# A routed block of convolution, attention and experts: b1 in a constant channel, GELU in two halves, both 16-bit casts on ScalarE

## The reference

```python
x = x + conv_block(group_norm(x))         # 3x3 depthwise, BN, ReLU, prune; 1x1, BN, ReLU, prune
t = tokens(x)                             # 12544 tokens of 128 channels
t = t + spike_attention(layer_norm(t))    # causal, within an image of 784 tokens
flat = layer_norm(t)
logits = flat @ Wr                        # 8 experts, the best two of each token
for e in range(8):
    hdn = gelu(flat @ W1[e] + b1[e])      # 128 -> 512, exact GELU
    y = hdn @ W2[e] + b2[e]               # 512 -> 128
    out += gates[:, e:e+1] * y
```

## Time and profile before

| | us |
|---|---|
| median of 3 runs | 878.62 |
| the three runs | 872.77, 878.62, 881.32 |
| the profiled execution, its own time | 872.08 |
| its span, first to last instruction | 870.4 |
| TensorE busy in it | 714.3 (82%) |
| VectorE busy | 658.5 (76%) |
| GpSimd busy | 512.9 (59%) |
| ScalarE busy | 413.2 (47%) |
| mean granted TensorE clock | 0.926 of full |

### The profile page before, as it was taken

The page is one execution under the profiler, slowest core; times in us unless marked ns, Lnnn a source line. Parts: engine busy times, 40 slices in busy tenths (PEclk is TensorE's granted clock), DMA queues, the critical chain, the costliest instruction groups (busy, mean ns, idle before and its releaser), DMA issues. The chain is left out here.

```text
span 870.4 us, 21192 instructions
## 1 busy us (share of the span) xinstructions
PE 714.3 (82%) x6445; PEld 554.3 (64%) x6445; DVE 658.5 (76%) x1980; ACT 413.2 (47%) x922; POOL 512.9 (59%) x500
## 2 busy tenths in 40 slices
PE   1579999999999999798488977669999999995433
PEld 0245666666566666566377866658899999994322
DVE  2647888888888887877759867747888888885666
ACT  0245465566665666455456544335555555552000
POOL 4100057777767776676556677777677777776000
PEclk9989999999999999999679998889999999998555
DMA  7201213232323232122163333325854454441997
GB/s 161 61 19 61 63 59 97 90 113 90 112 88 117 93 117 70 31 73 70 51 108 79 74 76 70 79 72 126 106 95 93 95 95 88 89 84 48 292 306 260
DMA packets 123065, 86.44 MB, mean 99 GB/s; under 512 B 96492, under 2 KB 105232, under 8 KB 122979
## 3 DMA queue, kind: packets, MB, share of 16 engines
q1 hardware_dynamic: 106066, 52.86, 26.2%
q0 software_dynamic: 13888, 26.03, 10.5%
q10 hardware_dynamic: 3024, 6.43, 2.0%
HBM read 30.50 MB, written 35.48 MB: 76 GB/s over the span
## 5 line engine op out<-in xcount | busy, mean ns | idle before, releaser
L477 POOL DMA_INDIRECT expert_rows<-xb_x,dest x210 | 230.5, 1098 | 83.6 <-issue 53.1
L466 POOL DMA_INDIRECT dispatched_rows<-rows,pos x224 | 216.9, 968 | 95.9 <-issue 66.0
L720 PE MATMUL pair_d<-w,xb_x 128*128 x2520 | 177.4, 222 | 0.1
L521 PE MATMUL pair_a<-padx,tap_diag 128*128 128x392 f16 x864 | 164.7, 338 | 0.9 <-ACT h L802 0.9
L720 PEld LDWEIGHTS pair_d<-w,xb_x 128*128 128x128 f16 x2520 | 157.9, 99 | 5.7 <-issue 0.2
L1305 DVE TENSOR_TENSOR xb_x<-seen_g,xb_x 128x512 f16<-128x512 f32 x210 | 137.3, 693 | 0.0
L521 PEld LDWEIGHTS pair_a<-padx,tap_diag 128*128 128x128 f16 x864 | 83.6, 100 | 58.0 <-issue 3.9
L884 ACT ACTIVATE seen_g<-pair_b,b 128x256 f32<-128x256 f32 x212 | 83.4, 477 | 63.7 <-PE pair_b L704 50.0
L884 ACT ACTIVATE seen_g<-pair_c,b 128x256 f32<-128x256 f32 x208 | 82.0, 477 | 34.9 <-PE pair_c L704 33.8
L1302 DVE CAST xb_x<-seen_g 128x512 f16<-128x512 f32 x210 | 84.6, 444 | 0.4 <-ACT seen_g L884 0.3
L704 PE MATMUL pair_b<-xrt,w 128*128 128x256 f16 x636 | 80.6, 278 | 3.4 <-DMA xrt<-dispatched_rows 3.4
(11 more groups left out here) (208 smaller groups left out, 1127.0 us busy)
## 6 DMA issues: line engine op xcount, KB each, us to landing
xb_x<-in_x SPq DMA_DIRECT2D x32, 392.0 KB, 4.2
w<-expert_rows SPq DMA_DIRECT2D x16, 784.0 KB, 6.5
t_all<-t SPq DMA_DIRECT2D x16, 392.0 KB, 3.2
out<-w ACTq DMA_DIRECT2D x16, 392.0 KB, 5.3
w_stage<-in_L_ffn_W SPq DMA_DIRECT2D x16, 256.0 KB, 4.4
dispatched_rows<-rows,pos POOLq DMA_INDIRECT x224
expert_rows<-xb_x,dest POOLq DMA_INDIRECT x210
dispatched_rows<-pad_rows SPq DMA_DIRECT2D x16, 131.0 KB
```

Of the source, the lines that this page charges most:

```text
L466: pool.indirect_dma_start(xs, bass.IndirectOffsetOnAxis(ap=pos[:, u, t, k:k + 1].bitcast(U32), axis=0), rows[:, u, t, :].bitcast(U32), Non ...
L477: pool.indirect_dma_start(ys, bass.IndirectOffsetOnAxis(ap=dest[:, half, slot, s:s + 1].bitcast(U32), axis=0), y[:, slot, s, :], None, bou ...
L521: last = T.matmul(pa[:, h * BANK:h * BANK + HALF], tap_diag[:, wp, tap, :], padx[:, xp, u, ky + 14 * h:ky + 14 * h + 14, kx:kx + SIDE], st ...
L720: last = T.matmul(dst, ghl[:, t % 2, gp, f * TILE + s * P:f * TILE + (s + 1) * P], w2[:, wp, bass.ds(w0 + f * P, P)], start=False, stop=(f ...
```

## The change

b1 no longer goes in as a bias operand of the GELU. The rows' last channel becomes the constant 1, and b1 takes the place of that channel's weights:

- A layer-normed row sums to zero over its channels. The second norm now shifts by the token's last channel instead of its mean, so channel 127 would be 0 and the other channels are off by a constant. `norm_rows` writes 127 channels; `xf` was filled with ones at the start.
- W1 is centred: its mean over the channels, made by a matmul with `avg_all` (`weight_mean`, one fp32 matmul of 512 columns), is subtracted by VectorE from its first 127 rows (`centre_weights`). That takes the constant out again.
- SP writes b1[n] over row 127 of the staged W1, after the mean was taken.

All weights are now loaded at the start, in 16 DMAs of 256 KB, into the last third of `t2_all`, which the images from the sixth on overwrite later (SP waits in step 8 for the last low halves). Mean, centring, high and low halves of expert n are made in step n+1, so in steps 1 to 8, all of which are unrolled now (LOOP_FROM is 10). The turning of b1 and ScalarE's expert registers are gone.

With no bias that differs between quarters, `gelu` takes two quarters at once: two GELUs of 512 columns. The two casts of 512 columns move from VectorE's `split` to ScalarE's new `high_half`, which follows `gelu` in its program and takes over the wait for output(t-2).

The core of the diff:

```diff
-POOL_CONSTS = 27
-W_LOADS = 18
+POOL_CONSTS = 28
+W_LOADS = 17
+GELU_HALF = FC // 2
+WEIGHTS_FROM, WEIGHTS_TO = 1, E + 1
-LOOP_FROM, LOOP_TO = 6, IMAGES - 2
+LOOP_FROM, LOOP_TO = 10, IMAGES - 2
+        staged = t2_all[:, IMAGES * L - 2 * E * HID:IMAGES * L].rearrange("p (n e h) -> p n e h", n=2, e=E)
...
+            for e in range(E):
+                sp.dma_start(staged[:, 0, e, :], a["L1_ffn_W1"][e]).then_inc(S["stage_loaded"], 16)
+                sp.dma_start(staged[:, 1, e, :].rearrange("p (f d) -> p f d", f=FC),
+                             a["L1_ffn_W2"][e].rearrange("(f p) d -> p f d", p=P)).then_inc(S["stage_loaded"], 16)
...
+                if with_weights(step):
+                    n = step.k - WEIGHTS_FROM
+                    sp.wait_ge(S["w_mean"], n + 1)
+                    sp.dma_start(staged[P - 1:P, 0, n, :], a["L1_ffn_b1"][n:n + 1]).then_inc(S["b1_loaded"], 16)
+                    if n == E - 1:
+                        sp.wait_ge(S["w_lo_ready"], 2 * E)
...
+            const(G.memset(xf[:], 1.0))
...
+            def weight_mean(n):
+
+                pe.wait_ge(S["stage_loaded"], 32 * E)
+                T.matmul(pc[:, BANK:2 * BANK], avg_all[:], staged[:, 0, n, :], start=True, stop=True).then_inc(S["w_mean"], 1)
...
                 if norm:
                     group_mean(norm[0])
+                if with_weights(step):
+                    weight_mean(step.k - WEIGHTS_FROM)
...
-                act.wait_ge(S["stage_loaded"], 32 * j + 32)
-                A.activation(w1[:, 0, bass.ds(j * HID, HID)], w_stage[:, 0, :], ACT.Copy, scale=WSCALE).then_inc(S["w_hi_ready"], 1)
-                A.activation(w2[:, 0, bass.ds(j * HID, HID)], w_stage[:, 1, :], ACT.Copy, scale=WSCALE).then_inc(S["w_hi_ready"], 1)
+                act.wait_ge(S["w_centred"], j + 1)
+                act.wait_ge(S["b1_loaded"], 16 * j + 16)
+                A.activation(w1[:, 0, bass.ds(j * HID, HID)], staged[:, 0, j, :], ACT.Copy, scale=WSCALE).then_inc(S["w_hi_ready"], 1)
+                A.activation(w2[:, 0, bass.ds(j * HID, HID)], staged[:, 1, j, :], ACT.Copy, scale=WSCALE).then_inc(S["w_hi_ready"], 1)
...
             def gelu(t):
-                c0 = experts[t] * FC
                 hp = (pb, pc)[t % 2]
                 if some(2 * (t - 1)):
                     act.wait_ge(S["ghl_ready"], 2 * (t - 1))
-                for f in range(FC):
-
-                    act.wait_ge(S["h_ready"], FC * t + 2 * (f // 2) + 2)
-                    A.activation(g[:, t % 2, f, :], hp[:, f * TILE:(f + 1) * TILE], ACT.Gelu, scale=1.0 / WSCALE,
-                                 bias=b1[:, bass.ds(c0 + f, 1)]).then_inc(S["g_ready"], 1)
+                for h in range(2):
+
+                    act.wait_ge(S["h_ready"], 2 * t + h + 1)
+                    A.activation(half_of(g, t, h), hp[:, h * BANK:(h + 1) * BANK], ACT.Gelu, scale=1.0 / WSCALE).then_inc(S["g_ready"], 1)
+
+            def high_half(t):
+                if some(t - 1):
+                    act.wait_ge(S["y_ready"], t - 1)
+                for h in range(2):
+                    act.wait_ge(S["g_ready"], 2 * t + h + 1)
+                    A.activation(ghl[:, t % 2, 0, h * 2 * TILE:(h + 1) * 2 * TILE], half_of(g, t, h), ACT.Copy).then_inc(S["g_hi_ready"], 1)
...
+                if step.image(4):
+                    last_channel = pair[0:TT, 0:NT * P].rearrange("p (t c) -> p c t", c=P)[:, P - 1, :]
+                    V.scalar_tensor_tensor(out=shift[0:TT, NT:GN], in0=last_channel, scalar=-1.0, in1=rstd[0:TT, NT:GN],
+                                           op0=ALU.mult, op1=ALU.mult)
...
+            def centre_weights(j):
+
+                dve.wait_ge(S["w_mean"], j + 1)
+                V.tensor_tensor(staged[0:P - 1, 0, j, :], staged[0:P - 1, 0, j, :], pc[0:P - 1, BANK:2 * BANK], ALU.subtract).then_inc(S["w_centred"], 1)
...
             def split(t):
 
-                if some(t - 1):
-                    dve.wait_ge(S["y_ready"], t - 1)
-                for h in range(2):
-                    dve.wait_ge(S["g_ready"], FC * t + 2 * h + 2)
-                    V.tensor_copy(ghl[:, t % 2, 0, h * 2 * TILE:(h + 1) * 2 * TILE], gv(t, h)).then_inc(S["g_hi_ready"], 1)
                 for h in range(2):
                     dve.wait_ge(S["g_hi_ready"], 2 * t + h + 1)
```

More of the change, by code:

```diff
@@ L257, in steps, with with_weights @@
                 body(Step(k, k // 2, k % 2))
+        def with_weights(step):
+            return isinstance(step.k, int) and WEIGHTS_FROM <= step.k < WEIGHTS_TO
         def table(engine, entries, t, count, most):
@@ L295, in body @@
                 j = step.j
-                if step.u == 0 and step.image(0):
-                    if some(2 * j):
-                        sp.wait_ge(S["w_lo_ready"], 2 * j)
-                    sp.dma_start(w_stage[:, 0, :], a["L1_ffn_W1"][bass.ds(j, 1)].rearrange("a d h -> d (a h)")).then_inc(S["stage_loaded"], 16)
-                    sp.dma_start(w_stage[:, 1, :].rearrange("p (f d) -> p f d", f=FC),
-                                 a["L1_ffn_W2"][bass.ds(j, 1)].rearrange("a (f p) d -> p (a f) d", p=P)).then_inc(S["stage_loaded"], 16)
+                if with_weights(step):
[4 more added lines that the diff above has]
+                        sp.wait_ge(S["w_lo_ready"], 2 * E)
                 if step.image(3):
@@ L598, in attend @@
                     pe.wait_ge(S["gvar_ready"], i + 4)
+                if with_weights(step):
+                    pe.wait_ge(S["w_centred"], step.k - WEIGHTS_FROM + 1)
                 for h in range(2):
@@ L803, in second_relu, with norm_rows @@
                              scale=bn[:, 1, 6:7], bias=bn[:, 1, 7:8]).then_inc(S["h2_ready"], 1)
-            def norm_rows(out_, pair, n0, ts, done):
+            def norm_rows(out_, pair, n0, ts, done, width=P):
                 for t in ts:
-                    last = A.activation(out_[:, t, :], pair[0:TT, t * P:(t + 1) * P], ACT.Identity,
+                    last = A.activation(out_[:, t, 0:width], pair[0:TT, t * P:t * P + width], ACT.Identity,
                                         scale=rstd[0:TT, n0 + t:n0 + t + 1], bias=shift[0:TT, n0 + t:n0 + t + 1])
@@ L848, in body @@
                     see(att[0])
-                if norm and step.u == 0:
-                    high_weights(step.j)
+                if with_weights(step):
+                    high_weights(step.k - WEIGHTS_FROM)
                 if step.normed():
@@ L889, in gate_tanh @@
                 A.activation(tanh[:, half, :, :], arg[:, half, :, :], ACT.Tanh).then_inc(S["tanh_ready"], 1)
[L891 to L899 removed]
             gelu(0)
+            high_half(0)
             gate_tanh(0, 0)
[L902 removed]
             gelu(1)
+            high_half(1)
             for t in range(TILES):
@@ L1056, in variances, with scales @@
                 V.tensor_scalar(var[0:TT, 0:GN], ln[:, 4, :], 1.0 / P, EPS, ALU.mult, ALU.add).then_inc(S["var_ready"], 1)
-            def scales(link, step):
+            def scales(link, step, pair):
                 dve.wait_ge(S["root_ready"], step.k + 1)
@@ L1169, in body @@
                     group_variance(norm[0])
+                if with_weights(step):
+                    centre_weights(step.k - WEIGHTS_FROM)
                 if att:
@@ L1180, in body @@
                     variances(norm_link, step)
-                    scales(norm_link, step)
+                    scales(norm_link, step, pd)
                 if att:
                     add_attention(*att)
-                if norm and step.u == 1:
-                    low_weights(step.j)
+                if with_weights(step):
+                    low_weights(step.k - WEIGHTS_FROM)
                 if isinstance(step.k, int) and step.k == 0:
@@ L1340, in _ @@
                         norm_link.n = DVE_STEPS["norm"] - 4
-                        scales(norm_link, step)
+                        scales(norm_link, step, pa)
                     if t == at + 4:
```

44 lines of the change are left out of this document (17 added, 27 removed).

## The result

The changed kernel takes 872.7 us (median of 20 runs, 868.1 to 874.8) where the kernel before takes 878.8 beside it (20 runs, 872.8 to 884.0): ratio 0.9924, 95% interval 0.9907 to 0.9941, 6.1 us or 0.8% faster. The forecast was 871.6, and the time lies in its class of "within 1%". A second measurement of the same two kernels, among the experiments, gave 870.9 against 877.2: 0.9921 [0.9893, 0.9949].

What follows compares the result with a forecast made beforehand. No single engine: VectorE late in the tiles' first stretch, GpSimd binding the middle, TensorE the last. Tile stage -7.7, start -2.8, means +5.8, shift +1.1, collisions -3.1, unrolling -0.3: -7.0 us, so 871.6 us, range 861 to 884.

Steps and rivals of the forecast that it cites:

- within 1%: Whole kernel: time within about 1% (8.8 us) of the kernel before, what a measurement can tell from no change; chance 0.52.
- Start: Start of the first stage: ScalarE's root no longer waits behind a weight load; 2.8 us gained, at the bad end 9 lost.
- Rival C: Step 1: the up-front weights are late and TensorE stands 12 us; 5 us lost, 884 us; chance 0.10.
- Means: Steps 3 to 8: each mean over W1 costs TensorE 0.97 us; 5.8 us lost in six steps.
- the added shift: Second norm, 14 steps: one added small instruction of 0.17 us before norm_ready, half of it showing; 1.1 us lost.
- Collisions: Steps 5, 7, 9 and 13: the masking of weights no longer stretched from 0.29 to 1.05 us; 3.1 us gained.
- Tile stage, first stretch: First nine tiles, where VectorE is late: relieved of 8 us of casts, 3 us gained (bounds 0 and 6).
- Middle stretch: Tiles where GpSimd sets the end: half of the 5.3 us by which stores are stretched; 2.7 us gained (0 to 5.3).
- Last stretch: Last 74 tiles, where TensorE sets the end: the 2 us over TensorE's own pace gained.
- Rival D: Tile stage: ScalarE becomes the bound of a tile at 3.1 us; 11 us lost, 890 us; chance 0.08.
- A: Tile stage: casts are all of GpSimd's stretch and VectorE's relief shows in full; 13.3 us gained, 866 us; chance 0.20.
- B: Tile stage gains only the 2 us at its end, as the sends alone bind GpSimd; 877 us; chance 0.14.

Runs made afterwards that it cites:

- spread sends: Changed kernel with the 28 sends of the held images one to every second tile from tile 9 to 63: 1.0019 to the kernel before, with TensorE held up.
- means-out kernel: Changed kernel without the eight means over W1 and without the centring: 0.9949 to the kernel before, with TensorE held up.

## Why the prediction came out right, and where it didn't

**Start: right.** Root at 19.51 (19.8 forecast), the mean at 28.88 (by 29), no wait for the weights. By the root of step 2 the kernel is 3.4 us ahead (54.16 against 57.53); 2.8 were forecast. Rival C, the late weights, is out.

**Means: right in place, too large.** 0.63 us a step and not 0.97 between the roots of steps 5 and 8, 0.9 between the roots of steps 3 and 4. Steps with one are 24.03 us (24.3 forecast). So the term of 5.8 measured about 4 (six times 0.63, and 0.3 for the one step that took 0.9). VectorE's centring cost nothing that shows, and neither did the added shift: steps without a mean last 23.4 us as before. The 1.1 us for it measured 0.

**Collisions: the old ones as forecast, and a new one that I named only as a sign.** Steps 5, 7, 9 and 13 won 4 x 0.77 = 3.1 us. But in step 4 the masking now meets GpSimd's row subtraction, and that step is 3.4 us longer than before, 2.8 of it past the mean. The failed step is that I followed where the mean pushes the masking against one of GpSimd's two subtractions, and not against the other. It is a narrow thing: six times in the traces the row subtraction began 0.04 us behind the masking, which then took 1.95 us, and four times it began 0.07 to 0.08 behind and the masking took 0.29. Where it isn't held step 4 lasts 25.1 us (subtractions of 16 columns) or 24.9 (mask on ScalarE), so about 1.8 of the 2.8 us are this collision. About 1 us is left in both, with the one-column instruction at 1.60 us in both; that this is its price wasn't tested. With the mask on ScalarE step 14 lasts 23.5.

The first stage ends 0.2 us later than before (first gating product at 450.38 against 450.17), where the terms made 0.7 later; this stage's total came near because of errors on both sides.

**Tile stage, first stretch: right in kind, half the size.** The row positions come at 481.1 instead of 483.2, 2.1 us earlier (forecast 3), and the stretch gained 1.5 to 2.

**Middle stretch: wrong.** 2.7 us were forecast from half of the stores' stretch; it gained 0. I had the right bound (GpSimd), and sized the casts' part of its stretch wrongly: the failed step is "Half, 2.7". What decides is not what lies beside a store but what VectorE has under way as it begins. A store that begins at least 0.05 us into a subtraction or a cast lasts until 0.85 us after the end of that instruction, if that is more than 0.97 us; every other store lasts 0.97. By this 204 of the 210 stores of before come out within 0.03 us, and 209 of the changed kernel's (two of before take 1.90 and are not explained). Here is one store of the kernel before, then two of the changed kernel (each with VectorE's timeline above GpSimd's):

```profile
610.90 0.80 DVE L1302 CAST xb_x<-seen_g 128x512 f16<-128x512 f32 x2
611.62 1.28 DVE L1305 TENSOR_TENSOR xb_x<-seen_g,xb_x 128x512 f16<-128x512 f32 x2
...
611.43 1.12 POOL L477 DMA_INDIRECT expert_rows<-xb_x,dest  x1 [0.31 <-issue]
```

```profile
606.67 1.29 DVE L1328 TENSOR_TENSOR xb_x<-seen_g,xb_x 128x512 f16<-128x512 f32 x2 [0.24 <-ACT xb_x L912]
...
606.46 0.97 POOL L484 DMA_INDIRECT expert_rows<-xb_x,dest  x1 [0.30 <-issue]
...
481.53 1.28 DVE L1328 TENSOR_TENSOR xb_x<-seen_g,xb_x 128x512 f16<-128x512 f32 x2
...
482.19 1.48 POOL L484 DMA_INDIRECT expert_rows<-xb_x,dest  x1 [1.70 <-DVE xb_x L1346]
```

At 611.43 a cast was under way and the subtractions came 0.2 us later; at 606.46 they came 0.2 us later with no cast ahead, and the store wasn't stretched. At 482.19 the second subtraction had just begun.

Of the 26.4 us by which the 210 stores of before exceed 0.972 each, 18.3 lie on 60 stores that a subtraction held and 7.2 on 46 that a cast held. But in the middle stretch only 3 of the 38 stores fell on a cast, 0.2 us of 4.1. That is what I should have counted instead of taking half. Without the casts the whole excess is 13.7 us: the casts' 7.2 are gone, and the subtractions hold 63 stores for 13.6. In the middle stretch the subtractions' part stayed (3.4 and 3.3 us), the stores' mean hardly moved (1.08 to 1.06 us) and that of the 28 sends rose, 0.99 to 1.02.

The Trainium skill, "SBUF — State Buffer", section "Who interferes with whom", says that a VectorE instruction with two SBUF inputs contends with a GpSimd instruction that reads SBUF, and one with at most one, outside the two-port modes, doesn't. The runs agree for the subtraction: 1.04 us a store with two, 0.973 with one. In which mode the casts ran no trace shows. The prediction's "if a store only writes descriptors" is not borne out, since the subtractions do hold stores. The row at 654.56 had said so the earlier trace rows, and I gave it half a weight.

**Last stretch: right.** 2.6 us against 2, at TensorE's own pace: the products are 2.76 us apart in the median in both traces, the tiles 2.85 on average instead of 2.89. Rival D, ScalarE as the bound, is out where TensorE isn't held up: 2.2 us of ScalarE's work a tile. With TensorE held up something like it happens, since the casts are better on VectorE there. What in ScalarE's chain costs it is not settled.

**Rivals A and B, and the total.** A is out, as the casts hold 7.2 of the stores' 26.4 us. B had the middle stretch at nothing, as it came, but for a reason that the runs refute: the sends alone don't bind GpSimd at 89 us, since without the stores' stretch it takes 84.0 and 84.5. The tile stage gained 4 us where 7.7 were forecast, and the two traces differ by 2.3 us where the terms made 7.0. That the median came within 1.1 us of the forecast is thus partly luck.

**Open.** Which part of the tile stage's 4 us is the casts' and which the wide GELUs', since the kernels that undo one of them ran only with TensorE held up; whether the spread sends would win; why stage 3 lasts 69.7 to 74.3 us in kernels that are alike there; and 3.7 of the 6.1 us of the medians, which the two traces don't show.

## What to carry to other kernels

Work taken off an engine that isn't the bound pays only through what it was colliding with, so first find the colliding instruction: for each stretched instruction look up what the neighbour engine had under way as it began, and count these cases in the stretch that matters. With one operand in PSUM VectorE's subtractions no longer held GpSimd's indirect transfers, which gave 4.6 to 4.9 us where GpSimd is the bound; but the tiles behind lost 5.5, so price the longer hold on the bank first. And when an edit shifts a step by less than a microsecond, slide it against each large instruction of the neighbour engine, not only against the one it collides with now.

## What the runs showed of the hardware

- A store (indirect transfer issued by GpSimd) takes 0.97 us. If a 512-column VectorE subtraction with both inputs in SBUF, or a cast, was under way as it began, it lasts until 0.85 us after that one's end, up to 1.50 us in the changed kernel's two traces. One that begins behind the store's start leaves it at 0.97. With one of the subtraction's inputs in PSUM, none of 210 took over 1.01. The subtraction itself takes 0.68 to 0.69 us in both forms.
- Ahead of the 128th indirect transfer GpSimd stands 2.60 us for nothing that the profile names, in every trace and with or without a hardware loop.
- VectorE's 128-column masking takes 0.29 us, 1.95 when one subtraction of GpSimd began 0.04 us behind it, and 4.13 beside two in a row. The same on ScalarE takes 0.40, inside GpSimd's padding subtraction too.
- ScalarE's neighbouring instructions overlap by a quarter of a narrow one: four GELUs of 256 columns take 1.56 us, 0.39 each, where one is 0.48 long.
- Where TensorE was held up nothing is different until about 125 us. Then TensorE stands between matmuls of one convolution with no releaser, and its clock falls. Here are four windows of the means-out kernel (busy us of PE, PEld, DVE, ACT, POOL, then clock, DMA, GB/s) and TensorE's waits from 200 to 300 us:

```profile
0.00:120.00 120.00, 83.29 (x466) 52.64 (x467) 78.41 (x269) 48.41 (x88) 24.43 (x45) 0.97 0.34 92
193.00:197.70 4.70, 1.99 (x8) 0.61 (x7) 1.40 (x7) 0.00 (x0) 3.48 (x5) 1.00 0.16 49
197.70:208.00 10.30, 6.09 (x21) 3.27 (x22) 6.62 (x24) 5.34 (x11) 3.07 (x4) 0.50 0.23 71
200.00:300.00 100.00, 77.50 (x433) 47.87 (x432) 58.35 (x212) 43.62 (x85) 48.02 (x47) 0.86 0.19 61
...
PE pair_a L532 <- issue: 18.7, 22, 2.3
```
